# GpSimd takes the second norm's root iterations and the last additions of the row sums

## The reference

```python
xn = (x - mean(x)) / sqrt(var(x) + 1e-5)
# attention branch
Q, K, V = relu(xn @ Wq + bq), relu(xn @ Wk + bk), relu(xn @ Wv + bv)
mask = sign(abs(sum(xn, axis=-1)))       # rows and keys with a row sum of exactly 0 are masked
attn = softmax(masked_causal(Q K^T / sqrt(8))) * mask
s = gamma * norm(attn @ V + xn) + beta
# expert branch
mu, var = mean(xn), mean((xn - mu)**2)
x2 = (xn - mu) * rsqrt(var + 1e-5) * ln_scale + ln_bias      # the second norm
xa = x2 @ attn_w.T + attn_b + xn
h = gelu(xa @ w1[e] + b1[e]);  eo = h @ w2[e] + b2[e]
g = gelu(eo @ next_w.T + next_b)
out = x + s * silu(g)
```

## Time and profile before

| | |
|---|---|
| median of 3 runs | 526.83 us (526.4 to 527.27) |
| profiled execution, its own time | 526.47 us |
| its span, first to last instruction | 524.7 us |
| PE busy in the span | 437.2 us (83%) |
| DVE busy | 399.6 us (76%) |
| ACT busy | 302.1 us (58%) |
| POOL busy | 126.5 us (24%) |
| granted TensorE clock, mean | 0.942 |

### The profile page before, as it was taken

The page is one execution under the profiler, slowest core; times in us unless marked ns, Lnnn a source line. Parts: engine busy times, 40 slices in busy tenths (PEclk is TensorE's granted clock), DMA queues, the critical chain, the costliest instruction groups (busy, mean ns, idle before and its releaser), DMA issues.

```text
span 524.7 us, 10282 instructions
## 1 busy us (share of the span) xinstructions
PE 437.2 (83%) x3697; PEld 269.2 (51%) x3697; DVE 399.6 (76%) x976; ACT 302.1 (58%) x644; POOL 126.5 (24%) x346
## 2 busy tenths in 40 slices
PE   0049545999999559999999999999999999999980
PEld 0026334767667425555555556556556555555540
DVE  6989998899984267667977877877877877787606
ACT  0029134888787504556666567567567566666670
POOL 8000000000000021011155154164163163162281
PEclk9999957999999955899999999999999999999996
DMA  8900021244443200122312312213323213222000
GB/s 231 296 0 0 11 71 31 60 122 125 126 126 82 81 6 24 51 69 49 93 48 69 92 49 79 82 48 90 74 47 101 61 48 111 52 48 67 3 22 20
DMA packets 27433, 37.60 MB, mean 72 GB/s; under 512 B 5622, under 2 KB 19830, under 8 KB 27382
## 3 DMA queue, kind: packets, MB, share of 16 engines
q1 hardware_dynamic: 27382, 36.94, 25.9%
HBM read 25.91 MB, written 10.49 MB: 69 GB/s over the span
## 4 chain that ended last, share of the span: by engine, by line
PE 53%; DVE 9%; issue 1%; ACT 1%; DVEq 0%; ACTq 0%
PE banks L963 15%; PE banks L994 14%; PE banks L982 12%; PE banks L965 5%; PE banks L984 5%; DVE mx L816 5%; PE banks L1004 1%; DVE stats L863 1%; DVE aggr L867 1%; ACT pt L934 0%; DVE bits L69 0%; DVE seed L70 0%; PE banks L972 0%; DVE half L894 0%; DVE res L850 0%
## 5 line engine op out<-in xcount | busy, mean ns | idle before, releaser
L816 DVE TENSOR_REDUCE mx<-banks 128x1 f32<-128x384 f32 (+3 forms) x384 | 211.1, 597 | 63.6 <-PE banks L965 58.4
L934 ACT ACTIVATE pt<-banks 128x512 f32<-128x512 f32 (+2 forms) x384 | 184.8, 528 | 110.8 <-PE banks L984 99.9
L965 PE MATMUL banks<-causal,ident_b 128*128 128x128 bf16 x512 | 106.8, 228 | 0.0
L984 PE MATMUL banks<-causalT,ident_b 128*128 128x128 bf16 x512 | 103.8, 222 | 0.0
L963 PE MATMUL banks<-k_own,q_own 73*128 73x512 bf16 (+3 forms) x256 | 75.3, 331 | 11.2 <-DVEq L896 8.6
L994 PE MATMUL banks<-pt,vg 128*18 128x512 f32 (+3 forms) x1024 | 82.4, 440 | 0.5 <-ACT pt L934 0.5
L963 PE MATMUL banks<-w_room 73*128 73x512 bf16 (+3 forms) x256 | 69.0, 302 | 3.4 <-DVE mx L816 3.4
L982 PE MATMUL banks<-q_own,k_own 76*128 76x512 bf16 (+3 forms) x256 | 71.1, 310 | 0.0
L982 PE MATMUL banks<-w_room 76*128 76x512 bf16 (+3 forms) x256 | 67.7, 300 | 1.2 <-ACT pt L934 1.2
L726 POOL TENSOR_SCALAR mneg<-mx 128x16 f32<-128x16 f32 x32 | 8.1, 253 | 192.7 <-DVEq L824 192.7
L965 PEld LDWEIGHTS banks<-causal,ident_b 128*128 128x128 bf16 x512 | 52.1, 102 | 0.0
(11 more groups left out here) (155 smaller groups left out, 581.1 us busy)
## 6 DMA issues: line engine op xcount, KB each, us to landing
k_scratch<-parts SPq DMA_DIRECT2D x40, 128.0 KB, 2.4
q_own<-q_scratch SPq DMA_DIRECT2D x48, 96.0 KB
k_own<-k_scratch SPq DMA_DIRECT2D x48, 96.0 KB
w_room<-q_scratch SPq DMA_DIRECT2D x48, 96.0 KB
w_room<-k_scratch SPq DMA_DIRECT2D x48, 96.0 KB
q_scratch<-parts SPq DMA_DIRECT2D x24, 128.0 KB, 2.4
w_room<-in_w_dram SPq DMA_DIRECT2D x1, 2048.0 KB, 9.2
out_dram<-mixed SPq DMA_DIRECT2D x7, 256.0 KB, 2.5
```

What stands on the lines that cost most here:

```text
L816: ins = dve.tensor_reduce(mx[:, u % 2, heads[0]:heads[-1] + 1, q], banks[:, S0 + c % RING, 0:w * len(heads)].rearrange("p (h k) -> p h k", ...
L934: act.activation(weights(k, heads[0], len(heads)), banks[:, ST0 + j % RING, 0:(T - P * k) * len(heads)], ACT.Exp, scale=SCALE).then_inc(ex ...
L965: ins = mm(o[:, w - P:w], ident_b[:, :], causal[:, :], start=False, stop=True)
L984: ins = mm(o[:, 0:P], ident_b[:, :], causalT[:, :], start=False, stop=True)
```

## The change

VectorE keeps the variance and the seed of the second root (`second_seeds`) and signals `seeds_ready`; of the row sums it keeps the reduction to 16 lanes, which is no longer linked and signals `lanes_ready` by itself. GpSimd does the Newton steps (`second_roots`), the four additions, and the shift (`totals`), and signals `sums_ready`. ScalarE takes the scale from `y2` and the shift from `shift` instead of from `norm2`. The flags are made for all tiles at once in `masks`, behind the loop over batches and before the last batch's `rests`; it waits for all eight `sums_ready`.

```diff
--- before.py
+++ after.py
@@ -185,7 +185,7 @@
         qhi = s1("qhi", [P, TB, C])
         qlo = s1("qlo", [P, TB, C])
         xl_st = s1("xl_st", [P, 2, TB, C])
-        norm2 = s1("norm2", [P, B, 2, TB])
+        shift = s1("shift", [P, NT])
         xnT = s1("xnT", [P, 2, T])
         xlT = s1("xlT", [P, T])
         xaT = s1("xaT", [P, T])
@@ -208,6 +208,7 @@
         blank, consts = sem("blank"), sem("consts")
         dve_self, act_self = sem("dve_self"), sem("act_self")
         xn_ready, sums_ready = sem("xn_ready"), sem("sums_ready")
+        lanes_ready, seeds_ready = sem("lanes_ready"), sem("seeds_ready")
         xl_ready = sem("xl_ready")
         trx_done, trl_done = sem("trx_done"), sem("trl_done")
         q_done, k_done, v_done = sem("q_done"), sem("k_done"), sem("v_done")
@@ -224,7 +225,7 @@
         mask_ready, maskT_done, maskT_ready, mask_out = (sem(n) for n in (
             "mask_ready", "maskT_done", "maskT_ready", "mask_out"))
 
-        mean, var, a, y, t, s, sh, sl, r, nr, rem, v2, y2 = (small[:, k, :] for k in range(13))
+        mean, var, a, y, t, s, sh, sl, r, nr, rem, v2, y2, t2 = (small[:, k, :] for k in range(14))
 
         with nc.Block() as block:
             @block.sync
@@ -304,6 +305,40 @@
                     link(pool.tensor_copy(bias_rows[on_p, :, :], bias_part[on_p, p]))
                 pool.sem_inc(bias_ready, 1)
 
+                tt = pool.tensor_tensor
+
+                def second_roots(tok, group):
+
+                    at = slice(group[0], group[0] + group[1])
+                    pool.wait_ge(seeds_ready, tok.next(seeds_ready))
+                    for _ in range(3):
+                        link(tt(t2[:, at], y2[:, at], y2[:, at], ALU.mult))
+                        link(tt(t2[:, at], t2[:, at], v2[:, at], ALU.mult))
+                        link(pool.tensor_scalar(t2[:, at], t2[:, at], -0.5, 1.5, ALU.mult, ALU.add))
+                        link(tt(y2[:, at], y2[:, at], t2[:, at], ALU.mult))
+
+                def totals(tok, i):
+
+                    at = slice(TB * i, TB * i + TB)
+                    pool.wait_ge(lanes_ready, tok.next(lanes_ready))
+                    v = s16[:, at, :].rearrange("p n (a b l) -> p n a b l", a=2, b=2)
+                    link(tt(s8[:, at, :, :], v[:, :, :, 0, :], v[:, :, :, 1, :], ALU.add))
+                    link(tt(s4[:, at, :], s8[:, at, 0, :], s8[:, at, 1, :], ALU.add))
+                    v = s4[:, at, :].rearrange("p n (a b) -> p n a b", b=2)
+                    link(tt(s2[:, at, :], v[:, :, :, 0], v[:, :, :, 1], ALU.add))
+                    link(tt(rem[:, at], s2[:, at, 0], s2[:, at, 1], ALU.add))
+                    link(pool.tensor_scalar(shift[:, at], rem[:, at], -1.0 / C, None, ALU.mult))
+                    link(tt(shift[:, at], shift[:, at], y2[:, at], ALU.mult))
+                    pool.sem_inc(sums_ready, 1)
+
+                tok = Tokens(pool)
+                for i in range(B):
+                    if i == 0:
+                        second_roots(tok, GROUPS[0])
+                    if i == 2:
+                        second_roots(tok, GROUPS[1])
+                    totals(tok, i)
+
                 pool.sem_inc(blank, -12)
 
             @block.vector
@@ -374,25 +409,28 @@
                         link(ins)
                     dve.sem_inc(xn_ready, 1)
 
-                def second_roots(group):
+                def second_seeds(group):
 
                     at = slice(group[0], group[0] + group[1])
                     link(dve.tensor_scalar(v2[:, at], var[:, at], 1.0 / C, None, ALU.mult))
                     link(tt(v2[:, at], v2[:, at], r[:, at], ALU.mult))
                     link(tt(v2[:, at], v2[:, at], r[:, at], ALU.mult))
                     link(dve.tensor_scalar(v2[:, at], v2[:, at], 1e-5, None, ALU.add))
-                    rsqrt_newton(link, dve, y2[:, at], t[:, at], v2[:, at], 3)
+                    rsqrt_newton(link, dve, y2[:, at], t2[:, at], v2[:, at], 0)
+                    dve.sem_inc(seeds_ready, 1)
 
                 def sums(i):
 
                     tiles = slice(TB * i, TB * i + TB)
-                    row_sum(link, dve, rem[:, tiles], s16[:, tiles, :], s8[:, tiles, :, :], s4[:, tiles, :],
-                            s2[:, tiles, :], xn_all[:, tiles, :])
-                    link(dve.scalar_tensor_tensor(out=norm2[:, i, 1], in0=rem[:, tiles], scalar=-1.0 / C,
-                                                  in1=y2[:, tiles], op0=ALU.mult, op1=ALU.mult))
-                    link(dve.tensor_copy(norm2[:, i, 0], y2[:, tiles]))
-                    dve.sem_inc(sums_ready, 1)
-                    link(dve.tensor_scalar(zero_all[:, tiles], rem[:, tiles], 0.0, None, ALU.is_equal))
+                    dve.tensor_reduce(s16[:, tiles, :], xn_all[:, tiles, :].rearrange("p n (k l) -> p n l k", l=16),
+                                      AX.X, ALU.add).then_inc(lanes_ready, 1)
+
+                def masks():
+
+                    dve.wait_ge(sums_ready, B)
+                    link(dve.tensor_scalar(zero_all[:, :], rem[:, :], 0.0, None, ALU.is_equal))
+                    link(dve.tensor_scalar(live_all[:, :], zero_all[:, :], -1.0, 1.0, ALU.mult, ALU.add))
+                    dve.tensor_scalar(mask_b[:, :], zero_all[:, :], -BIG, None, ALU.mult).then_inc(mask_ready, 1)
 
                 def rests(tok):
 
@@ -421,7 +459,7 @@
                 variances(GROUPS[0])
                 roots(GROUPS[0])
                 quotients(0)
-                second_roots(GROUPS[0])
+                second_seeds(GROUPS[0])
                 sums(0)
                 quotients(1)
                 sums(1)
@@ -434,13 +472,11 @@
                     quotients(i)
                     rests(tok)
                     if i == 2:
-                        second_roots(GROUPS[1])
+                        second_seeds(GROUPS[1])
                     sums(i)
-                    if i == B - 1:
-                        link(dve.tensor_scalar(live_all[:, :], zero_all[:, :], -1.0, 1.0, ALU.mult, ALU.add))
-                        dve.tensor_scalar(mask_b[:, :], zero_all[:, :], -BIG, None, ALU.mult).then_inc(mask_ready, 1)
                     gate(tok, i - 2)
                     lows(tok)
+                masks()
                 rests(tok)
                 gate(tok, B - 2)
                 lows(tok)
@@ -457,7 +493,8 @@
                     act.wait_ge(sums_ready, tok.next(sums_ready))
                     for k in range(TB):
                         ins = act.activation(xl_st[:, i % 2, k, :], xn_all[:, TB * i + k, :], ACT.Identity,
-                                             bias=norm2[:, i, 1, k:k + 1], scale=norm2[:, i, 0, k:k + 1])
+                                             bias=shift[:, TB * i + k:TB * i + k + 1],
+                                             scale=y2[:, TB * i + k:TB * i + k + 1])
                     ins.then_inc(xl_ready, 1)
 
                 def norm_out(tok, n):
```

## The result

The changed kernel takes 527.77 us (median of 16 runs, 526.8 to 529.49), the kernel before 526.43 (16 runs, 525.5 to 527.63): ratio 1.0029, 95% interval 1.0018 to 1.0040. It is slower, as forecast, but by 1.3 to 1.5 us and not by 3.3.

The account below looks back on a forecast made before the run. VectorE was taken to bound the part before attention (busy 147.6 of 183 us), TensorE close behind. Terms 1.9+3.35-2.0=+3.25 us on the 526.83 median gave 530.1 us, range 523.5 to 537.5.

Parts of the forecast that it names:

- 11x0.34: First group: eleven GpSimd instructions left beside VectorE's short ones, one let through for each, some 0.34 us apiece.
- the last batch's tail: Time behind the settled periods, at the last batch: left at nothing, 0.5 us either way.
- The first head, +1.9 us: First group, batch 0: ScalarE's second norm starts 2.35 us late, so group two's big row sum starts 1.9 us later.
- Rival one (groups of four): VectorE's short instructions shut GpSimd out in groups of four: batch 0 sums at 38.9, total 537.9 us; chance 0.25.
- signs of being wrong: Second norm on time, small GpSimd instructions keeping 0.2 us beside two-input ones, or the settled period moving the other way.
- The second head, +3.35: Second group, batch 2: nine GpSimd instructions left at 0.36 us; ScalarE starts 4.05 us late, costing 3.35 us.
- The cost of the clock: TensorE's return to full clock after the longer wait before batch 2: up to 2 us added, left in the range.
- The settled batches, -2.0: Batch 3's reduction to batch 7's: loop of 11.08+D, period taken as 14.2 instead of 14.71 us, four times.
- The coin that I had left open: Settled batches: GpSimd's last instruction just makes it before low k (D=2.85) or waits for it (3.4).
- D: Settled batches: delay from the reduction's end until ScalarE starts the second norm, forecast 2.85 or 3.4 us.
- hardly hindered: Rival: GpSimd's small operands slip through beside VectorE, D is 1.9, total -2.9, 523.9 us; chance 0.18.
- The longer settled period: Rival: low k and quotient stand right behind the reduction, D is 4.7, period 15.8, total 536.5 us; chance 0.07.

Follow-up runs that it names:

- c: Changed kernel with the Newton steps and the whole sums of batches 0 and 2 back on VectorE: 523.17 us, ratio 0.9935 to the kernel before.
- f: Changed kernel with six Newton steps instead of three on GpSimd: 535.30 us, ratio 1.0166 to the kernel before.
- e: Changed kernel with VectorE waiting until GpSimd has the sums of batches 0 and 2: 525.37 us, ratio 0.9975 to the kernel before.
- a_same: The changed kernel run again without any edit: 527.64 us, ratio 1.0028 to the kernel before.
- the first trace: The changed kernel's first profiled execution, before the experiments: 526.8 us, the shortest of its sixteen runs.

## Why the prediction was right in direction and more than twice too large

The mechanism was right: two late starts against a gain in the settled batches. What failed are two steps of the sum: the price of GpSimd's instructions beside VectorE's short ones ("11x0.34" and "nine are left at 0.36"), and the last batch's tail, put at nothing. The paragraphs go through the prediction's terms one by one.

*VectorE's saving goes into waiting at batches 0 and 2.* Right: 6.0 and 6.1 us of idle time there, 6 predicted. c and f show that these two starts turn a gain of 3.2 us into a loss.

*GpSimd is held up by two-input instructions.* Right. All engines together, around the first root, with the starts of GpSimd's (POOL) and VectorE's (DVE) instructions:

```profile
28.70 0.68 DVE L398 TENSOR_TENSOR quo<-xn_all,small 128x512 f32<-128x512 f32 x1
28.91 0.53 POOL L315 TENSOR_TENSOR small<-small 128x8 f32<-128x8 f32 x1
29.41 0.43 DVE L399 TENSOR_SCALAR qhi<-quo 128x512 int32<-128x512 int32 x1
29.51 0.38 POOL L316 TENSOR_TENSOR small<-small 128x8 f32<-128x8 f32 x1
29.87 0.69 DVE L400 TENSOR_TENSOR qlo<-quo,qhi 128x512 f32<-128x512 f32 x1
29.98 0.65 POOL L317 TENSOR_SCALAR small<-small 128x8 f32<-128x8 f32 x1
30.60 1.14 DVE L407 SCALAR_TENSOR_TENSOR gate_all<-qhi,small,xn_all 128x128 f32<-128x128 f32 x4
30.71 0.30 POOL L318 TENSOR_TENSOR small<-small 128x8 f32<-128x8 f32 x1
31.09 0.20 POOL L315 TENSOR_TENSOR small<-small 128x8 f32<-128x8 f32 x1
```

28.91 to 29.44, 29.51 to 29.89 and 29.98 to 30.63: each ends 0.05 to 0.07 after the VectorE instruction beside it, the one-input L399 over int32 included. Here the Trainium skill, SBUF — State Buffer, "Who interferes with whom", covers both: two SBUF inputs shut out GpSimd's reads, and so does a one-input VectorE instruction that takes both ports; the trace agrees, as far as L399 is such a one: it goes through 512 columns in 0.43 us, the two-input ones beside it in 0.69. Experiment e shows the hold-up as the cause of 4.1 us of the late starts.

*The first head, +1.9 us: mis-sized.* a_same has +1.32. The term that failed is "11x0.34, with 0.2 for the wider first addition" beside the short instructions. No row gave the 0.34: one for each short instruction would have been 0.294, since four and the gap behind them take 1.175 (in the kernel before two groups of four start at 34.77 and 35.95). One more had come through by then, and the ten left took 3.1 us, from 31.09 to 34.19. What they take is one for each short instruction: 31.09, 31.37, 31.66, 31.94, 32.27, four in 1.18 us, and a group of four short ones with its gap takes 1.175. f shows the same over sixteen (31.27 to 35.97, four times 1.175). So the prediction's rule was right there and its price wrong. Alone, in e with VectorE standing, four of these take 1.14 and the same ten 2.85, so the slowing is 0.03 an instruction: the two paces happen to be nearly the same. Rival one (groups of four) is out, 38.9 against 34.28. One of the prediction's signs of being wrong came in part: beside the short ones most GpSimd instructions keep 0.20 to 0.25 us. The start was 1.79 us late in a_same and not 2.35.

*The second head, +3.35: mis-sized for a like reason, "nine are left at 0.36".* +2.97. Eleven instructions instead of nine had come through when the short ones began at 88.23, and the seven left took 0.33 each and not 0.36; the start was 3.50 late on VectorE's clock, not 4.05; a little of it came back as slower TensorE passes (10.94 against 10.77 from start to parts before). The cost of the clock, up to 2 us, that I had only left in the range, came to +0.17 here and to -0.15 in the first trace. It does not follow the length of the wait: the way took 10.77 in f, where TensorE had waited 10.3 us, and 11.99 in e, where it had waited 3.9.

*The settled batches, -2.0: right.* -2.25. The coin that I had left open falls alternately: D is 2.74 in one batch and 3.21 in the next. With 3.21 my loop gives 11.08+3.21=14.29, which is measured. With 2.74 it gives 13.82, and measured are 14.01: there VectorE does not wait for the parts, but is late itself, because it had waited for the middle part of k before, and it goes through its two subtractions without a gap.

```profile
134.17 0.69 DVE L446 TENSOR_TENSOR parts<-rest,parts 128x512 bf16<-128x512 f32 x1 [1.15 <-ACT parts L554]
...
142.91 1.53 DVE L439 TENSOR_TENSOR rest<-full,parts 128x512 f32<-128x512 f32 x2
```

Then the two cases of D. In the first case GpSimd's last instruction passes before low k; in the second it waits for it (0.66 us instead of 0.20). GpSimd's first two of a batch:

```profile
103.37 0.63 POOL L325 TENSOR_TENSOR s<-s 128x32 f32<-128x32 f32 x1 [12.69 <-DVE s L425]
104.08 0.73 POOL L326 TENSOR_TENSOR s<-s 128x16 f32<-128x16 f32 x1
```

0.63 behind the gate, 0.73 behind low q, as predicted. TensorE's limit was read wrongly, 13.93 for 13.66, which did not matter to the forecast because D, or VectorE behind the middle part of k, held the period above both.

*"The last batch's tail I leave at nothing": this failed, the largest single miss.* It is -0.66. From batch 7's reduction to the last key parts the kernel before needs 171.72-157.93=13.79 us, since ScalarE waits for the stores of the previous parts, 0.39 us for q and 1.64 for k:

```profile
170.46 0.69 ACT L498 ACTIVATE full<-banks,cols_sb 128x512 f32<-128x512 f32 x1 [1.64 <-DMA k_scratch<-parts]
```

After it is 171.80-158.86=12.94, which is my own loop, 1.03+2.74+6.77+2.4. The settled loop runs a fifth time up to the parts, and I counted four.

So the sum 1.9+3.35-2.0=+3.25 should have read 1.32+2.97-2.25-0.66=+1.38. Four misses of 0.25 to 0.66 us (0.58, 0.38, 0.25, 0.66) all had the same sign, and the sum was a difference of larger numbers: +5.25 of loss against 2 of gain. The margin for the direction was thin: by the prediction's own measure, break-even lay at a mean step of 0.36 us, and the two groups came out at 0.357 and 0.457, so that the second one carried it. Of the rivals, "hardly hindered" has a half of the truth: beside the short instructions it nearly holds in time, beside those of 512 columns it does not, and D is 2.7 to 3.2 and not 1.9. The longer settled period is out (14.15 on average).

## What to carry to other kernels

An engine that is busy 80% of a stage can still be early at a few places, and the stage's time may hang on just these: here two starts, 1.8 and 3.5 us late, decide against 14 us of relief. When small work goes to GpSimd, ask what VectorE runs beside it: here the ones of 512 columns stretched its 0.20 to 0.25 us to 0.38 to 0.79 each, reductions and those of 128 columns hardly slowed it, so put the handed-over work beside a reduction, or let VectorE stand still if it would wait anyway. Hand over what is needed late (the root, which runs beside the row sum) and keep what is needed at once.

## What the runs showed of the hardware that was not expected

- Beside back-to-back two-input VectorE instructions of 128 columns GpSimd's small ones got in once for each, and the slower of the two set the step. With 8 columns that was VectorE: four in 1.175 us, where GpSimd alone takes 1.14 (f_roots6 and e_yield). With 24 columns it was GpSimd: four in 1.25 (f_roots6, 92.91 to 94.16), 1.24 alone, and VectorE's group of four then took 1.245 instead of 1.175. Beside VectorE instructions of 512 columns each took up to 0.79 us instead of 0.20 to 0.25.
- TensorE's way from the second norm to the key parts took 10.41 to 11.63 us in batch 0 and 10.62 to 11.99 in batch 2 over the traces of all these kernels, by when its passes returned from half to full speed after a wait; in batch 0 the granted clock read 1.00 in the shortest and in the longest. What sets the moment is open. The changed kernel's shortest run (526.8 us, 10.42 and 10.62) and a_same's (528.04 us, 11.09 and 10.94) differ by 1.0 us on these two ways, so that much of the spread of its runs (526.8 to 529.5) comes from here.
